# Attention layers computed densely over tiles of edge counts instead of over gathered edges

## The reference

```
L0  mean over a node's sources, a linear layer, relu
L1  three attention layers with 4 heads of 32 features. In each:
      xs = h @ Ws ;  a_s = sum(xs * att_s) ;  a_d = sum((h @ Wd) * att_d)   per head
      e = leaky_relu(a_s[src] + a_d[dst], 0.2)
      ex = exp(e - segment_max(e, dst)) ;  alpha = ex / (segment_sum(ex, dst) + 1e-16)
      h = segment_sum(xs[src] * alpha, dst) + bias      (relu between layers)
L2  PNA: mean, max, min and std of messages, three scalings, a linear layer, batch norm
L3  two rounds of mean over sources
```

## Time and profile before

| engine | busy us | share | instructions |
|---|---|---|---|
| PE (matmul) | 4016.0 | 81% | 21002 |
| DVE | 3777.7 | 76% | 10209 |
| ACT | 2452.5 | 49% | 5562 |
| POOL | 2774.1 | 56% | 2853 |

### The profile page before, as it was taken

The page is one execution under the profiler, slowest core; times in us unless marked ns, Lnnn a source line. Parts: engine busy times, 40 slices in busy tenths (PEclk is TensorE's granted clock), DMA queues, the critical chain, the costliest instruction groups (busy, mean ns, idle before and its releaser), DMA issues.

```text
span 4975.7 us, 70568 instructions
## 1 busy us (share of the span) xinstructions
PE 4016.0 (81%) x21002; PEld 2278.1 (46%) x21002; DVE 3777.7 (76%) x10209; ACT 2452.5 (49%) x5562; POOL 2774.1 (56%) x2853
## 2 busy tenths in 40 slices
PE   6999796888888568888865888888389999977799
PEld 3444344444444334444433444444267767644444
DVE  8999885898888769888885988888677777774211
ACT  5888703454454255545433554545366666663100
POOL 0000033777777677777767777777367777772000
PEclk9999897899998779999986999989699999987899
DMA  4444561344444334444432444444266777761566
GB/s 168 158 155 156 196 242 48 106 137 131 133 125 134 97 106 141 127 134 127 133 124 64 133 135 133 126 134 129 76 198 234 238 241 242 236 208 63 212 244 216
DMA packets 358410, 763.69 MB, mean 153 GB/s; under 512 B 73631, under 2 KB 274751, under 8 KB 357316
## 3 DMA queue, kind: packets, MB, share of 16 engines
q1 hardware_dynamic: 238396, 547.19, 29.9%
q0 software_dynamic: 89744, 193.14, 14.9%
q10 hardware_dynamic: 29944, 19.32, 1.5%
HBM read 392.63 MB, written 366.78 MB: 153 GB/s over the span
## 4 chain that ended last, share of the span: by engine, by line
POOL 30%; PE 16%; DVE 16%; issue 14%; DMA 7%; ACT 5%; POOLq 0%; SPq 0%; DVEq 0%; ACTq 0%
POOL big L776 28%; PE psT L1149 7%; DVE big L1911 3%; DMA big<-table,src_win 3%; DMA src_bc<-pe_src_d 2%; DVE big L1826 2%; DVE big L1925 2%; PE psT L1291 2%; PE psY L1291 1%; DVE big L1901 1%; PE psY L1405 1%; DVE big L1850 1%; PE psL L1291 1%; ACT hT L967 1%; POOL start_ad L744 1%
## 5 line engine op out<-in xcount | busy, mean ns | idle before, releaser
L776 POOL DMA_INDIRECT big<-table,src_win x2604 | 2512.3, 965 | 870.9 <-issue 760.9
L1911 DVE SCALAR_TENSOR_TENSOR big<-big,keep_win 128x132 f32<-128x132 f32 x2184 | 782.8, 358 | 77.8
L953 ACT ACTIVATE hT<-src_bc,node_c 128x640 bf16<-128x640 f16 x840 | 621.2, 814 | 146.9 <-PE psL L1291 83.8
L982 ACT ACTIVATE psH<-d_b 128x60 f32<-128x60 f32 x168 | 37.6, 224 | 1171.0 <-DVE d_b L1893 1171.0
L1291 PE MATMUL psT<-big 128*128 128x408 bf16 x1800 | 490.3, 338 | 55.0 <-DVE big L1826 55.0
L1291 PE MATMUL psT<-big,hT 128*128 128x408 bf16 x1200 | 374.8, 376 | 150.2 <-DVE big L1850 74.0
L1291 PE MATMUL psY<-big 128*128 128x408 bf16 x1800 | 490.0, 338 | 0.0
L958 ACT ACTIVATE hT<-hT 128x3200 bf16<-128x3200 bf16 x168 | 482.2, 2870 | 5.3
L1291 PE MATMUL psY<-big,hT 128*128 128x408 bf16 x1200 | 377.2, 379 | 103.6 <-DVE big L1850 67.8
L1826 DVE TENSOR_SCALAR big<-src_bc,node_c 128x640 bf16<-128x640 f16 x1260 | 407.5, 395 | 22.7 <-PE psL L1291 22.7
L728 POOL TENSOR_TENSOR dst_i<-big 128x512 f32<-128x512 f32 (+1 forms) x7 | 8.1, 1152 | 684.9 <-DMA big<-A_d 605.2
(11 more groups left out here) (372 smaller groups left out, 8323.4 us busy)
## 6 DMA issues: line engine op xcount, KB each, us to landing
rows<-big SPq DMA_DIRECT2D x168, 952.0 KB
big<-A_d SPq DMA_DIRECT2D x17, 6400.0 KB
rows<-big SPq DMA_DIRECT2D x112, 896.0 KB
A_d<-big SPq DMA_DIRECT2D x396, 200.0 KB, 1.9
big<-A_d SPq DMA_DIRECT2D x32, 1600.0 KB, 10.9
big<-table,src_win POOLq DMA_INDIRECT x2604
src_bc<-pe_src_d ACTq DMA_DIRECT2D x84, 128.0 KB
table<-big SPq DMA_DIRECT2D x15, 350.0 KB, 3.0
```

The costliest lines, as they stand in the source:

```text
L776: pool.indirect_dma_start(out=rows[:, k, 0:p.table_w], out_offset=None, in_=table, in_offset=bass.IndirectOffsetOnAxis(ap=src_win[:, s, k: ...
L953: ins = nc.scalar.activation(hot_of[t], src_bc[:, q % 2, :], ACT.Square, bias=node_c[:, t:t + 1], scale=-1.0)
L1911: v.scalar_tensor_tensor(state[:, k, 0:GATW], prev[k][:, 0:GATW], kw[:, 0, k:k + 1], rows[:, k, 0:GATW], ALU.mult, ALU.add).then_inc(chain ...
```

## The change

The three GAT passes go, with all that serves only them: the gathers and fetches of stage 3, `start_ad`, the scatter, `odd_src`, `links`, the running sums and the joining of lanes. `Pass` stays for PNA alone, written out without the cases. In place of the three passes stands a dense form over the counts of stage 1.

A layer has 8 chunks (`NCH`) of 400 targets (`CH`), and a chunk 25 tiles of 128 sources: 200 tiles of counts, 128x400, a layer. With a = a_s of the source (one per partition), d = a_d of the target (one per column) and v = d - shift, the logit is bent as max(0.8v, -0.8a) + 0.2v + a. For heads 0 and 1 GpSimd does the maximum (one `tensor_scalar` each) and the addition (one `tensor_tensor` over both heads); for heads 2 and 3 VectorE does max(v + 0.8a, 0.2v) in one instruction and 0.2a is left. ScalarE adds what is left of `a` as the bias of its exponential and writes one of two PSUM buffers (`psE`). VectorE multiplies by the counts. TensorE sums over sources: 33 columns of `xs_1` (32 features and a one, for the denominator) by 400 columns, f32, heads 0 and 2 at PSUM partition 0, heads 1 and 3 at 64, in two banks. Results lie in three buffers (`MOVING`).

The shift of a target is not its exact maximum. 32 levels between the smallest and the largest `a` are turned into powers of two, 25 bf16 matmuls a chunk add them over the sources that are present (the counts read as bf16), and the exponent of the sum tells the highest level. The small matrices of the next chunk (`levels`, `top_rows`, `spread_row`, `keep_rows`) are issued inside tiles 17 to 23, the division of the chunk before inside tiles 2 to 4.

SP loads the counts in halves (13 and 12 source tiles) into a ring of 3. `keep` is computed after attention, since its place holds buffers. The result has features on the partitions, so that the next layer can use it as it is; after the third, 25 transposes bring it back. GAT_EPS goes from 1e-16 to 1e-36, as the sums are shifted by a bound and not by the maximum. PNA, L3, the counts and L0 stay but for names, semaphores that are merged, and the memory map.

The core of the diff (removed passes left out):

```diff
+            for J in range(NH):                                   # SP: NH = 24
+                for late in range(2):
+                    k = 2 * J + late
+                    if k >= RING:
+                        sp.wait_ge(ring_used, k - RING + 1)
+                    sp.dma_start(a_half[k % RING][:, :, 0:q], A_d[a:a + CHB, :, HALF_W * late:HALF_W * late + q]...)
+                if J == 0:
+                    sp.wait_ge(pick_rdy, NBK)
+                    sp.dma_start(pick_d, pick[:]).then_inc(spilled, 16)
...
+            for n in range(NT * NH):                              # GpSimd
+                J, t = n // NT, n % NT
+                if t == 0:
+                    pool.wait_ge(row_rdy, H * J + 2)
+                if n >= MOVING:
+                    pool.wait_ge(summed, n - MOVING + 1)
+                for h in range(2):
+                    ins = pool.tensor_scalar(soft[n % MOVING][h], row_v[J % 2][:, 4 + h, :], s_all[:, 3, t, h:h + 1], None, ALU.max)
+                ins.then_inc(bent_p, 1)
+                pool.wait_ge(bent_p, 2 * n + 1)
+                pool.tensor_tensor(soft_2[n % MOVING], soft_2[n % MOVING], row_v[J % 2][:, 0:2, :]..., ALU.add).then_inc(bent_p, 1)
...
+                    for t in range(NT):                           # ScalarE
+                        for h in range(H):
+                            k = H * n + h
+                            if h == 0:
+                                act.wait_ge(bent_p, 2 * n + 2)
+                            elif h >= 2:
+                                act.wait_ge(bent_v, 2 * n + h - 1)
+                            if k >= 2:
+                                act.wait_ge(weight_rdy, k - 1)
+                            nc.scalar.activation(psE[k % 2], soft[n % MOVING][h], ACT.Exp,
+                                                 bias=s_all[:, 0 if h < 2 else 2, t, h:h + 1]).then_inc(soft_rdy, 1)
+                        if c and t == 4:
+                            layer_rows(g, J - 1)
+                        if c < NCH - 1 and 20 <= t < 20 + H:
+                            near_row(J + 1, t - 20)
+                    move_sums(J)
...
+                    for t in range(NT):                           # TensorE
+                        if t == 0 and J:
+                            pe.wait_ge(ev_rdy, 4 * J)
+                        if t == 23 and c < NCH - 1:
+                            keep_rows(J + 1)
+                        for a in range(2):
+                            pe.wait_ge(weight_rdy, H * n + 2 * a + 2)
+                            for k in range(2):
+                                ins = nc.tensor.matmul(acc[a][64 * k:64 * k + HC, 0:CH], xs_1[:, t, 2 * a + k, :], soft[n % MOVING][2 * a + k],
+                                                       start=(t == 0), stop=(t == NT - 1))
+                        ins.then_inc(summed, 1)
+                        if c and t == 2:
+                            shares(J - 1)
+                        if c < NCH - 1:
+                            if t == 17:
+                                levels(g, J + 1)
+                            if t == 18:
+                                top_rows(J + 1)
+                            if 19 <= t < 19 + H:
+                                spread_row(J + 1, t - 19)
...
+            def highest(J):                                       # VectorE
+                dve.wait_ge(lev_ps, 2 * J + 1)
+                link(v.tensor_single_scalar(bits.bitcast(I32), psH[:, 0:CH].bitcast(I32), 23, op=ALU.arith_shift_right))
+                v.tensor_scalar(bits, bits.bitcast(I32), float(LOW + STEEP), float(LOW), ALU.min, ALU.max).then_inc(near_rdy, 1)
+            def near(J):
+                dve.wait_ge(lev_ps, 2 * J + 2)
+                link(v.tensor_scalar(m_4, psH[0:H, 0:CH], ends_4[:, 3:4], ends_4[:, 5:6], ALU.mult, ALU.add))
+                link(v.tensor_tensor(v_4, m_4, psS[0:H, 0:CH], ALU.add))
+                link(v.tensor_scalar(v_4, v_4, 0.0, DEEPEST, ALU.max, ALU.min))
+                v.tensor_tensor(v_4, v_4, m_4, ALU.subtract).then_inc(near_rdy, 1)
+            def bend(n, h):
+                if n >= MOVING:
+                    dve.wait_ge(summed, n - MOVING + 1)
+                v.scalar_tensor_tensor(soft[n % MOVING][2 + h], psV[h], s_all[:, 1, t, 2 + h:3 + h], row_v[J % 2][:, 2 + h, :],
+                                       ALU.add, ALU.max).then_inc(bent_v, 1)
+            def weigh(n, h):
+                dve.wait_ge(soft_rdy, k + 1)
+                v.scalar_tensor_tensor(soft[n % MOVING][h]..., psE[k % 2]..., CAP, counts_of(J, t),
+                                       ALU.min, ALU.mult).then_inc(weight_rdy, 1)
+            def divide(J):
+                dve.wait_ge(share_ps, J + 1)
+                link(v.tensor_scalar(share, psH[:, 0:CH], GAT_EPS, None, ALU.add))
+                link(v.reciprocal(share, share))
+                v.tensor_tensor(share, share, psS[:, 0:CH], ALU.mult).then_inc(share_rdy, 1)
...
+                    for t in range(NT):
+                        # weigh 0, bend(n+1, 0), weigh 1, bend(n+1, 1), weigh 2, weigh 3
+                        tile_weights(n, t < NT - 1 or c < NCH - 1)
+                        if c and t == 3:
+                            divide(J - 1)
+                        if c < NCH - 1:
+                            if t == 17:
+                                highest(J + 1)
+                            if t == 18:
+                                near(J + 1)
+                    dve.wait_ge(summed, NT * (J + 1))
+                    for at in (0, 64):
+                        v.tensor_copy(ev[at:at + HC, 1, :], psZ[at:at + HC, 0:CH]).then_inc(ev_rdy, 1)
```

More of the change, by code:

```diff
@@ new lines, in gather @@
+                    for k in range(p.dma_steps(s)):
+                        pool.indirect_dma_start(
+                            out=rows[:, k, 0:p.table_w], out_offset=None, in_=table_d,
+                            in_offset=bass.IndirectOffsetOnAxis(ap=src_win[:, s, k:k + 1], axis=0)
+                        ).then_inc(gathered[s], 16)
+            gather(0)
+            with pool.Fori(1, p.rounds, 1) as rnd:
+                gather(rnd)
+            for r in range(ROWS_SLOTS):
+                pool.wait_ge(rows_out[r], p.groups // ROWS_SLOTS * 16)
@@ new lines, in middle @@
+            def middle(b):
+                act.wait_ge(rest_rdy, b + 1)
+                nc.scalar.copy(table_s[:, 5 * b:5 * b + 5, 1, :], rest_of[:, 5 * b:5 * b + 5, :]).then_inc(mid_rdy, 1)
+            for b in range(8):
+                if b < 7:
+                    keep_batch(2, b)
+                if b >= 1:
+                    rows_of(b - 1)
+                    if b >= 2 and b != 6:
+                        high(b - 2 if b < 6 else 4)
+            for b in range(NB):
+                middle(b)
@@ L1112, in _ @@
+            nc.scalar.activation(bn[:, 2, :], bn[:, 1, :], ACT.Sqrt, bias=eps[:, 0:1]).then_inc(bn_std, 1)
+            for b in range(NB + 1):
+                if b < NB:
+                    deviation(3, b)
+                if b:
+                    normal(3, b - 1)
+            keep_hT(3)
             for b in range(NBK + 2):
@@ L1422, in back_to_features @@
+            node_sum(NT - 2)
+            node_sum(NT - 1).then_inc(bn_ps, 1)
+            for t in range(NT):
+                n = P if t < NT - 1 else TAIL
+                pe.wait_ge(bn_sq_in, t // BT + 1)
+                ins = nc.tensor.matmul(psS[:, D:2 * D], ones[0:n, :], root[0:n, t, :], start=(t == 0), stop=(t == NT - 1))
+            ins.then_inc(bn_ps, 1)
+            to_features(3)
+            pe.wait_ge(hT_rdy, 7 * 4)
             def back_to_features(b):
```

1627 lines of the change are left out of this document (727 added, 900 removed).

## The result

The changed kernel takes 5345.5 us (median of 4 runs, 5341.0 to 5355.0) against 4972.3 for the kernel before: 1.0754 times its time (95% interval 1.0739 to 1.0770). The forecast was 4877, with 4680 to 5100 for 8 in 10. Both the sign and the size are wrong. The profiled execution has a span of 5353.2 us (before 4975.7).

A forecast was written before the change was run, and what follows sets the result against it. Before, engines waited in turn, none alone the bound; after, a VectorE-ScalarE loop of 3.30 us a step. Layers of 660+161+57.5=878.5 us, three 2635.5, start PNA 95 us earlier: span 4881, median 4877; 8 in 10: 4680 to 5100.

The forecast's parts named there:

- The maximum has no row: GpSimd's 400-column maximum had no priced example: bounds 0.46 to 1.03 us, taken as 0.5, GpSimd 2.9 us a step.
- the loop: VectorE's weigh 2, ScalarE's next exponential 0, then weigh 0: sets the step at 3.30 us, above VectorE's own 3.04.
- projections, settling, filling and the ends of layers: Added once per attention layer: projection 18 us, settle 14.5, filling the pipeline 15.5, end of last chunk 9.5; sum 57.5.
- Rival C: GpSimd becomes the bound: with a maximum at 1.03 us its step is 4.0, total 5150 us; chance 0.13.
- Rival D: VectorE operations that wait and signal do not overlap: step 3.81 us, 306 us more, total 5180; chance 0.10.
- ScalarE's exponential: Each of four a step over 400 columns: 0.585 us long, 0.54 apart, 2.2 us together, no bound.
- rival B: Exponentials of 0.3 us leave VectorE's 3.04 us step; paired narrow matmuls also shorten chunk waits: total 4680 us; chance 0.22.
- The chunk: Stalls that each chunk adds beside its 25 steps, seven times a layer: 23.0 us, 161 a layer.
- The frame: What lies around the attention layers; PNA was taken as unchanged at the old 1391 us.
- Weigh and bend have one SBUF tensor and PSUM, so they go free: VectorE's multiplication by counts (weigh) and its maximum for heads 2 and 3 (bend) are not slowed by GpSimd.
- The price of 1.5 us for the operations that do collide: Per chunk, one addition and two clampings of VectorE in highest and near are slowed by GpSimd: 1.5 us.
- I take no overlap: TensorE's two 33-column matmuls at different partitions run one after the other: 2.68 us a step, from 1.34 to 2.68.

The follow-up runs named there:

- the copies: Changed kernel with GpSimd's two maxima a step replaced by copies of the same 400 columns (heads 0 and 1 not bent): 4881.0 us, 0.9813 of before.
- Without maxima: Changed kernel with GpSimd's two maxima a step left out, its addition reading both rows directly (heads 0 and 1 not bent): 4881.2 us, 0.9816 of before.
- the spread order: Kernel without maxima, with VectorE's second bend moved from before weigh 1 to between weigh 2 and weigh 3: 4750.9 us, 0.9566 of before.
- the first kernel with one relu: Changed kernel with head 0's maximum moved to ScalarE as a relu, one tile ahead, head 1's left on GpSimd: 5078.4 us, 1.021 of before.

## Why the prediction was wrong, point by point

- **The step of the argument that failed** is the sentence "The maximum has no row", with its bounds: "upper as an addition: 1.03 ... so I take 0.5". Measured 1.28, above the upper end. It made GpSimd's sum 2.9 us, beside the 3.30 of the loop, where it is 4.48 and sets the step. With 0.5 put in its place (the copies) the kernel takes 4881.0 us; the forecast was 4877.
- That these two differ by 4 us is luck. Without maxima, from the first projection of attention to PNA's are 2662.5 us (forecast 2661.7), but the 600 steps take 28 us more than forecast, the chunks' stalls some 52 less, and projections, settling, filling and the ends of layers 25 more. The start of attention (forecast 828.3) says nothing to a few us: it lies between 823.6 and 828.5 in kernels whose code ahead of it is the same.
- Why the bounds failed: a maximum reads one tensor fewer than an addition, so I let an addition of the same columns bound it. No row said that GpSimd's prices are ordered by what is read. The rows behind 0.5 were an index and a selection, other instructions than the one to be priced. A copy does cost 0.51, so one-tensor operations have at least two prices.
- Rival C is what happened: GpSimd the bound, ScalarE and VectorE waiting for it, decided from 0.88 us a maximum. By its own way of counting it gives, with 1.28: step 4.48, of which 1.18x23 steps less 5 are paid, 22 us a chunk, 24 times: about 5410; the run has 5345. It had 0.13 and a price that ended at 1.03, so the range could not hold the result.
- The loop: 3.30 forecast, 3.35 measured without maxima, and 3.01 for VectorE's own 3.04 when the loop is opened. Right; it could show only where GpSimd's maxima were gone.
- VectorE's operations overlap: right (0.49 from weigh to bend, 0.54 from bend to weigh). Rival D falls.
- ScalarE's exponential: 0.589 to 0.598 long, 0.52 apart (0.585, 0.54). Right, so rival B's first half falls. B gives 4680, and the spread order shows that 3.01 is to be had by order alone.
- The chunk: 23.0 forecast, 19.6 measured where VectorE and ScalarE set the step (TensorE's wait 6.2 for 6.5), and only 10.6 in the changed kernel. There three buffers and GpSimd's head start hide part of each stall. 600x1.18=708 us more in the steps, about 21x(23.0-10.6)=260 less in the chunks; that leaves 448 of the 474 us by which the stage was longer than forecast.
- The frame: PNA's stage 1389.5 (1391). Right.
- The sentence "Weigh and bend have one SBUF tensor and PSUM, so they go free" held. The price of 1.5 us for the operations that do collide was low in the changed kernel: the second operation of "highest" takes 0.37 without maxima and a median of 1.59 with them, the clamping in "near" 0.36 and 2.04, together 2.9; the operation behind it, on two SBUF tensors, takes 0.56 in 22 of 24. GpSimd waits for sums behind both stalls (4.95 and 5.54 us around 1350), so it is likely that this is paid there in full; no run separates it.
- TensorE, "I take no overlap": wrong. It does not set the step; what it takes off a chunk's waits, as rival B has it, was not separated. See the last part.

## What to carry to other kernels

Price an operation on GpSimd from a row of the same instruction, or from a run of it alone; counting inputs does not bound it, and where no such row exists the range has to reach past the next dearer kind. Here GpSimd's sum lay 0.4 us under a step that runs 600 times, and two operations of unknown price were in it: 0.78 us too little for each decided the sign. An operation's place in a queue is a term as well: a relu one tile too late, with VectorE's old order, cost 0.5 us a step, a bend one place later won 0.3, and level sums spread over six tiles with the rows apart won 190 us.

## What the runs showed of the hardware

Two f32 matmuls of 33 output columns at partitions 0 and 64 run together. In the changed kernel (timeline, four records are two matmuls, two records one; then two windows with the granted clock ahead of the last two columns):

```profile
1214.08 0.83 PE L1197 MATMUL psS<-hT,w_att 128*4 128x400 f32 x2
...
1301.65 0.87 PE L1270 MATMUL psL<-pick,big 128*33 128x400 f32 x4 [2.10 <-DVE pick L1829]
...
1303.16 1.55 PE L1270 MATMUL psZ<-big 128*33 128x400 f32 x4 [0.64 <-DVE big L1829]
```

```profile
1297.00:1299.00 2.00, 1.18 (x6) 0.29 (x8) 1.63 (x4) 0.60 (x1) 1.92 (x2) 1.00 0.00 0
1303.00:1308.00 5.00, 3.41 (x10) 0.58 (x12) 3.21 (x7) 2.31 (x4) 4.92 (x4) 0.50 0.00 0
```

A pair takes 0.87 us in the window granted the whole 2.4 GHz and 1.55 in the one granted 0.50, 1.2 GHz; one after the other, two matmuls of 400 columns would take 1.34 and a tail at full clock by the earlier trace rows. Nor is a narrow matmul short by itself: a single one of 4 output columns takes 0.83 us where the window from 1214 to 1215 is granted the whole clock (first row). The Trainium skill (TensorE: Matmul & The Clock Gate, Part 3) says that column groups run concurrently; for f32 the trace agrees. Over the attention stage of the changed kernel the granted clock is 0.68, where TensorE waits 0.64 to 2.10 us ahead of a pair; even at 1.2 GHz its two pairs are 2x1.55=3.1 us of a step of 4.48, so the clock did not set the step.

A VectorE operation that collides with an addition of GpSimd's, and starts under it, ends just behind it. The conversion of 400 columns from SBUF to SBUF in "highest" (L1803) takes 1.59 us in the median in the changed kernel and 0.37 in each of its 24 executions with copies or without maxima:

```profile
1342.22 1.87 POOL L715 TENSOR_TENSOR pick<-pick,big 128x800 f32<-128x800 f32 x1
...
1342.51 1.80 DVE L1803 TENSOR_SCALAR lane_x<-lane_x 128x400 f32<-128x400 int32 x1
```

It ends at 1344.31, 0.22 us behind the addition. In the changed kernel 19 of the 24 start under an addition, and each ends 0.22 to 0.23 us behind it; two start under a maximum (L712) and take 0.38 and 0.40, three while GpSimd does nothing and take 0.37. Without maxima none of the 24 meets a GpSimd operation. So what sets its length is what GpSimd is doing just then, and not how busy it is on the whole. Under a maximum there is no one outcome: in the first kernel with one relu the clamping in "near" (L1825) starts under a maximum alone 20 times; 8 of them end 0.21 to 0.22 us behind it, 12 end before it. Why was not tried. GpSimd's own maxima keep within 30 ns (1267 to 1297) over 1200 executions all the while.
